# Second layer of the experts as three f32r products of split halves, with its weights split beforehand

## The reference

```python
def body(acc, ws):
    g, u, d, c = ws
    h = jax.nn.silu(x @ g.T) * (x @ u.T)
    return (acc + c[:, None] * (h @ d.T), None)
out, _ = jax.lax.scan(body, jnp.zeros_like(x), (gate_proj, up_proj, down_proj, coeff.T))
shared = jax.nn.silu(x @ shared_gate.T) * (x @ shared_up.T) @ shared_down.T
return (out + shared).reshape(B, S, Hd)
```

## Time and profile before

| | us |
|---|---|
| median of 3 runs | 1357.21 |
| lowest and highest run | 1356.95, 1358.68 |
| profiled execution | 1356.53 |
| its span | 1354.6 |
| TensorE busy in the span | 1297.6 (96%) |
| VectorE busy | 913.1 (67%) |
| ScalarE busy | 739.5 (55%) |
| GpSimd busy | 570.5 (42%) |

### The profile page before, as it was taken

How to read it: one execution, slowest core, us unless ns; L and a number is a source line. 1 busy time by engine, 2 the same in 40 slices (tenths; PEclk the granted TensorE clock), 3 DMA queues, 4 the chain that set the end, 5 groups by cost and what they waited for, 6 DMA issues and landing times.

```text
span 1354.6 us, 28636 instructions
## 1 busy us (share of the span) xinstructions
PE 1297.6 (96%) x8374; PEld 1162.2 (86%) x8374; DVE 913.1 (67%) x2131; ACT 739.5 (55%) x1688; POOL 570.5 (42%) x585
## 2 busy tenths in 40 slices
PE   7999999999999899999889999999989998989998
PEld 6898888989889797878778888988778997889996
DVE  6667666776766968687886666676767742346645
ACT  2556555565555545555546555555545654556653
POOL 5536545265330413122135546352000764656574
PEclk8999999999999899999999999999999998999999
DMA  3252645526352000000002111011157998999973
GB/s 122 87 179 85 205 142 179 178 85 205 128 182 97 28 5 28 5 28 21 13 20 67 43 62 66 27 51 54 63 188 266 393 344 302 313 383 392 390 246 113
DMA packets 128246, 195.97 MB, mean 145 GB/s; under 512 B 10400, under 2 KB 99744, under 8 KB 128160
## 3 DMA queue, kind: packets, MB, share of 16 engines
q1 hardware_dynamic: 64480, 109.77, 23.7%
q10 hardware_dynamic: 51392, 51.52, 11.2%
q0 software_dynamic: 12288, 33.57, 7.0%
HBM read 107.79 MB, written 87.03 MB: 144 GB/s over the span
## 4 chain that ended last, share of the span: by engine, by line
PE 73%; DVE 9%; issue 7%; DMA 5%; ACT 4%; SPq 1%; ACTq 0%; POOL 0%; DVEq 0%; POOLq 0%
PE ps_t L856 8%; PE ps_s L801 7%; PE ps_s L803 6%; PE ps_s L802 6%; PE ps_x L801 5%; PE ps_x L802 5%; PE ps_x L803 5%; PE ps_z L801 4%; DMA ring_down<-experts_dram 4%; PE ps_z L803 4%; PE ps_z L802 4%; PE ps_t L1021 3%; PE ps_z L1021 3%; PE ps_s L990 2%; PE ps_t L801 2%
## 5 line engine op out<-in xcount | busy, mean ns | idle before, releaser
L1133 ACT ACTIVATE prob<-prob,neg_max 128x128 f32<-128x128 f32 (+7 forms) x256 | 198.6, 776 | 243.4 <-DVE neg_max L1331 243.2
L1348 DVE TENSOR_TENSOR pT_lo<-ps_t,pT_hi 128x512 fp32r<-128x512 f32 (+2 forms) x320 | 189.5, 603 | 101.3 <-ACT pT_hi L1148 97.3
L1148 ACT ACTIVATE pT_hi<-ps_t 128x512 fp32r<-128x512 f32 (+2 forms) x320 | 161.1, 531 | 91.2 <-PE ps_t L856 91.1
L1331 DVE CUSTOM_DVE_ANT_0 prob<-ps_s,later_keys 128x128 f32<-128x128 f32 (+7 forms) x256 | 185.9, 748 | 2.4 <-PE ps_s L803 1.0
L856 PE MATMUL ps_t<-ident,prob 128*128 128x128 f32 x1152 | 172.3, 275 | 12.4 <-ACT prob L1133 5.7
L696 POOL DMA_INDIRECT xs<-xn,slots x128 | 127.7, 998 | 126.0 <-PE ps_z L1021 62.6
L856 PEld LDWEIGHTS ps_t<-ident,prob 128*128 128x128 f32 x1152 | 136.5, 141 | 39.0 <-DVE pT_lo L1348 6.7
L801 PE MATMUL ps_s<-k_hi,q_hi 128*128 128x512 f32 (+2 forms) x384 | 140.9, 367 | 1.0 <-DVE k_lo L1324 1.0
L801 PE MATMUL ps_s<-ring,a_hi 128*128 x384 | 127.0, 331 | 10.6 <-SPq L548 10.5
L1545 DVE TENSOR_TENSOR h<-sg,ps_s 128x256 f32<-128x256 f32 x112 | 47.1, 420 | 131.6 <-ACT sg L1182 131.3
L611 POOL TENSOR_TENSOR a_hi<-raw_a,zero 128x512 fp32r<-128x512 f32 x32 | 33.3, 1040 | 241.0 <-PE ps_x L803 156.0
(11 more groups left out here) (305 smaller groups left out, 3629.1 us busy)
## 6 DMA issues: line engine op xcount, KB each, us to landing
ring<-ws SPq DMA_DIRECT2D x56, 512.0 KB, 5.6
xs<-taken SPq DMA_DIRECT2D x16, 1536.0 KB, 9.7
xq<-xs ACTq DMA_DIRECT2D x48, 512.0 KB, 7.3
xs<-yq ACTq DMA_DIRECT2D x48, 512.0 KB, 7.6
ws<-split_to SPq DMA_DIRECT2D x34, 512.0 KB, 3.1
raw<-experts_dram SPq DMA_DIRECT2D x34, 256.0 KB, 3.3
raw_a<-w_a_dram SPq DMA_DIRECT2D x15, 512.0 KB, 3.7
ring_down<-experts_dram SPq DMA_DIRECT2D x56, 128.0 KB, 6.9
```

The source lines that it names most:

```text
L1133: act.activation(to, to, ACT.Exp, scale=-1.0, bias=neg_max[:, r:r + 1], accum_out=row_sum[:, c, j:j + 1]).then_inc(s_exp, 1)
L1148: act.activation(to, ps_t[m % 2][:, j * P:], ACT.Copy).then_inc(s_hi, 1)
L1331: dve.tensor_tensor_reduce(prob[r // BC][:, r % BC, 0:width(r)], ps_s[r % 2][:, first:first + width(r)], later_keys[:, S - width(r):], 1.0 ...
L1348: dve.tensor_tensor(lo, ps_t[m % 2][:, j * P:], hi.bitcast(F32), ALU.subtract).then_inc(s_bank_free, 1)
```

## The change

The second layer's weights are split together with the first layer's: `raw` takes all 768 columns of an expert, `split_to` and `ws` hold 768 high and 768 low columns, and a ring load reads high and low of both layers from `ws`, now 512 KB in rows of 2 KB and 256 KB in rows of 1 KB. `hT` becomes `hT_hi` (ScalarE's copy, in f32r) and `hT_lo` (a new subtraction on VectorE, from PSUM). TensorE's transposes of the next task, and the last second layer, wait for the low half. `down` calls `three`. To make room in SBUF the gather buffers go from 60 to 48, `coeff` shares `biased`, and two fillers go. Cut to its core:

```diff
-YQ, XQ, GATHERS = 4, 4, 60
+YQ, XQ, YG, GATHERS = 4, 4, 16, 48
...
-    ws = nc.dram_tensor("ws", [EX, P, 2 * GU], F32, kind="Internal").ap()
+    ws = nc.dram_tensor("ws", [EX, P, 2 * GU + 2 * D], F32, kind="Internal").ap()
...
-    coeff = sb("coeff", [P, NT, E])
+    coeff = biased
...
-        split_to = [sb(f"split_to{n}", [P, 2 * GU], F32R, attention) for n in range(2)]
-        raw = [sb(f"raw{n}", [P, GU], F32, attention) for n in range(2)]
-        sb("above_raw", [P, 1312], F32, attention)
+        split_to = [sb(f"split_to{n}", [P, 2 * GU + 2 * D], F32R, attention) for n in range(2)]
+        raw = [sb(f"raw{n}", [P, GU + D], F32, attention) for n in range(2)]
...
-    hT = [sb(f"hT{n}", [P, 2 * I])[:, :] for n in range(2)]
+    hT_hi, hT_lo = [[sb(f"hT_{w}{n}", [P, 2 * I], F32R)[:, :] for n in range(2)] for w in ("hi", "lo")]
...
-            sp.dma_start(ws[e], split_to[k % 2][:, 0:2 * GU].bitcast(F32)).then_inc(s_ws[k % 2], 16)
+            sp.dma_start(ws[e], split_to[k % 2][:, :].bitcast(F32)).then_inc(s_ws[k % 2], 16)
...
-                sp.dma_start(raw[k % 2][:, 0:GU], experts[e + 2][:, 0:GU]).then_inc(s_raw[k % 2], 16)
+                sp.dma_start(raw[k % 2][:, :], experts[e + 2]).then_inc(s_raw[k % 2], 16)
...
+        def by_part(t):
+
+            return t.rearrange("p (m c) -> p m c", m=2)
...
-            sp.dma_start(ring[slot].bitcast(F32), ws[which]).then_inc(s_ring[slot], 16)
-            sp.dma_start(ring_down[slot], experts[which][:, GU:]).then_inc(s_ring[slot], 16)
+            sp.dma_start(by_part(ring[slot].bitcast(F32)), by_part(ws[which])[:, :, 0:GU]).then_inc(s_ring[slot], 16)
+            sp.dma_start(by_part(ring_down[slot].bitcast(F32)), by_part(ws[which])[:, :, GU:]).then_inc(s_ring[slot], 16)
...
-            split(split_to[k % 2][:, 0:GU], split_to[k % 2][:, GU:2 * GU], raw[k % 2][:, 0:GU], count, s_pre)
+            split(split_to[k % 2][:, 0:GU + D], split_to[k % 2][:, GU + D:], raw[k % 2][:, :], count, s_pre)
...
-                pe.wait_ge(s_hT_out, g)
+                pe.wait_ge(s_hT_lo, g)
...
-                last = pe.matmul(to, hT[g % 2][:, at], downs[g][j],
-                                 start=what == "m" or j == 0, stop=what == "m" or j == 1)
+                last = three(to, hT_hi[g % 2][:, at], hT_lo[g % 2][:, at], downs[g][j][:, 0:D],
+                             downs[g][j][:, D:], what == "m" or j == 0, what == "m" or j == 1)
...
-                act.activation(hT[g % 2], ps_hT, ACT.Copy).then_inc(s_hT_out, 1)
+                act.activation(hT_hi[g % 2], ps_hT, ACT.Copy).then_inc(s_hT_out, 1)
...
+            elif kind == "B":
+                dve.wait_ge(s_hT_out, g + 1)
+                dve.tensor_tensor(hT_lo[g % 2], ps_hT, hT_hi[g % 2].bitcast(F32),
+                                  ALU.subtract).then_inc(s_hT_lo, 1)
```

More of the change, by code:

```diff
@@ L387, in build @@
     shared_gu = [sb(f"shared_gu{n}", [P, 2 * GU], F32R)[:, :] for n in range(NSH)]
-    shared_down = [sb(f"shared_down{n}", [P, D])[:, :] for n in range(NSH)]
-    down_cols = sb("ring_down", [P, RING * D])
-    ring_down = [down_cols[:, n * D:(n + 1) * D] for n in range(RING)]
+    shared_down = [sb(f"shared_down{n}", [P, 2 * D], F32R)[:, :] for n in range(NSH)]
+    down_cols = sb("ring_down", [P, RING * 2 * D], F32R)
+    ring_down = [down_cols[:, n * 2 * D:(n + 1) * 2 * D] for n in range(RING)]
     ring = [ring_cols[:, n * WC:(n + 1) * WC] for n in range(RING)]
-    later = sb("later", [P, 4 * D])
     with ExitStack() as routing:
         room_b1 = [sb(f"late_room{n}", [P, S], F32, routing) for n in range(3)]
-    yg = [sb(f"yg{n}", [P, D])[:, :] for n in range(24)]
+    yg = [sb(f"yg{n}", [P, D])[:, :] for n in range(YG)]
     yg += [t[:, d, n * D:(n + 1) * D].bitcast(F32) for t in (xT_hi, xT_lo) for d in range(ND) for n in range(S // D)]
-    yg += [t[:, n * D:(n + 1) * D] for t, count in ((later, 4), (above_ring, 4), (raw_a, 4)) for n in range(count)]
+    yg += [t[:, n * D:(n + 1) * D] for t, count in ((above_ring, 4), (raw_a, 4)) for n in range(count)]
     yg += [xn[:, t, :] for t in range(NT)]
@@ L450, in build @@
     s_gu, s_silu, s_h = sem("gu"), sem("silu"), sem("h")
-    s_hT, s_hT_out = sem("hT"), sem("hT_out")
+    s_hT, s_hT_out, s_hT_lo = sem("hT"), sem("hT_out"), sem("hT_lo")
     s_y, s_y_out, s_y_add = sem("y"), sem("y_out"), sem("y_add")
@@ L499, in _ @@
         for n in range(2):
-            sp.dma_start(raw[n][:, 0:GU], experts[n][:, 0:GU]).then_inc(s_raw[n], 16)
+            sp.dma_start(raw[n][:, :], experts[n]).then_inc(s_raw[n], 16)
             sp.sem_inc(s_ws[n], WS0)
@@ L561, in _ @@
         for n in range(NSH):
-            sp.dma_start(shared_gu[n].bitcast(F32), ws[E + n]).then_inc(s_shared, 16)
-            sp.dma_start(shared_down[n], experts[E + n][:, GU:]).then_inc(s_shared, 16)
+            sp.dma_start(by_part(shared_gu[n].bitcast(F32)), by_part(ws[E + n])[:, :, 0:GU]).then_inc(s_shared, 16)
+            sp.dma_start(by_part(shared_down[n].bitcast(F32)), by_part(ws[E + n])[:, :, GU:]).then_inc(s_shared, 16)
         sp.wait_ge(s_pv, PV0 + NP * TRS)
@@ L966, in gate_up @@
                 weights[g] = [ring_cols[:, bass.ds(a * WC, WC)] for a in at]
-                downs[g] = [down_cols[:, bass.ds(a * D, D)] for a in at]
+                downs[g] = [down_cols[:, bass.ds(a * (2 * D), 2 * D)] for a in at]
                 pe.wait_ge(s_w, second + (1 if b == 0 else 1 + E - RING))
@@ L1008, in down @@
             if g == NTASK - 1:
-                pe.wait_ge(s_hT_out, g + 1)
+                pe.wait_ge(s_hT_lo, g + 1)
             if g == 0:
```

## The result

The changed kernel takes 1375.32 us in the median (1373.63 to 1376.86, 4 runs) against 1357.36 us before: a ratio of 1.0131, 95% interval 1.0119 to 1.0143. It is 18 us slower; forecast were 1.9 us, and a range that ended at 1368. First the page of the changed kernel, its lines on the span, busy times, packets, SP's queue, and the loads of the ring (count, KB, median us from issue to landing).

What follows compares the result with a forecast made beforehand. TensorE was taken to set the pace except in early routing (VectorE) and two waits for weight loads (full DMA engines). Savings against loads and routing summed to +1.9 us: 1358.4 against 1356.53, 1359.1 as a median; range 1348 to 1368.

Steps and rivals of the forecast that it cites:

- The products: Second layer of each routed-expert task: six f32r products save 0.15 us, at most 16.8 us over 112 tasks, where TensorE leads.
- a rival: TensorE's products: weight loads set the pace, 0.38 us more per task, 42.6 us in all, 1399.8 us; chance 0.02.
- The subtraction just fits into these 0.45 us: VectorE beside routing, 1054 to 1090 us: the subtraction fits between routing step and next h; the 12.3 tasks gain nothing.
- between -1.8 and +1.8: Bounds in us on the 0 forecast for 1054 to 1090 us, 0.15 us per task either way.
- the second wait: TensorE waiting for weights, 1172.3 to 1212.8 us: 9 larger loads, 1.18 MB at 378 GB/s, +3.1 us.
- The first wait: TensorE waiting for weights, 1103.96 to 1143.5 us: 9 larger loads of 0.131 MB more at 346 GB/s, +3.4 us.
- the forecast 6.5: Larger ring loads in the two waiting stretches: 6.5 us more, as the DMA engines are full; bounds 0 and 16.0.
- Nothing that TensorE saves inside these two stretches counts: The two waiting stretches: TensorE's savings inside them bring nothing, since they end with a landing.
- The rival that the DMA engines lead there: After 1212.8 us: 14 larger loads come when wanted, +4.7 in place of 0, 1363.8 us; chance 0.14.
- The forecast's 0 for that stretch: 1212.8 to 1284 us: 0 taken between -3.6 (tasks' gain) and +4.7 (14 larger loads), as loads run ahead.
- The split and the buffers: Attention: the split's extra 7 us covered, 0. Gathers with 48 buffers: 0, at most 1.7 us.
- Queues that take turns: Ring loads: other queues keep their turns, so the waiting stretches grow by 16.0 in place of 6.5, 1368.6 us; chance 0.08.

Runs made afterwards that it cites:

- the run with routing steps behind: The changed kernel with each routing step placed behind the subtraction in VectorE's written order, not ahead of it: 1368.71 us, ratio 1.0088.
- the low half alone: The kernel before with 48 gather buffers, the subtraction and TensorE's waits for it; product still f32, loads as before, low half unused: 1364.23 us.
- the address arithmetic: The changed kernel with TensorE's addresses for gate and up worked out one step earlier, ahead of the transposes of h: 1374.32 us.
- The loads alone: The kernel before with 48 gather buffers and ring_down loaded as 256 KB instead of 128 KB, second copy unused: 1366.02 us, ratio 1.0072.
- the products alone: The changed kernel without subtraction or low-half loads, all products reading high halves; larger split and 48 gather buffers stay: 1352.09 us, ratio 0.9953.
- a third load in flight: The changed kernel with SP telling TensorE of a load two loads later, so three are in flight: 1369.50 us, ratio 1.0089.
- one transfer in fewer rows: The changed kernel with an expert's weights in one transfer of 768 KB in rows of 6 KB, 128 rows in place of 512: 1370.54 us.
- the run without the second sequence's stores: The changed kernel without the stores of the second sequence's results to HBM: 1367.17 us, ratio 1.0067.
- one run: The changed kernel with routing steps behind the subtraction, one load in rows of 6 KB and three loads in flight: 1373.46 us, ratio 1.0119.

## Why the prediction was wrong

**The products: right.** A task saves 0.15 us and takes 2.78 us where TensorE leads. With the low halves left out the products win 5.7 us. The Trainium skill (Perfetto Trace Analysis, Identifying the Most-Contended Engine) judges how much room TensorE has by the busy share of its weight loads, beside its share of peak arithmetic. As a sign of who leads the trace agrees: in the stretch of the tasks 48 to 57 they are busy for 24.88 of 25.43 us, before for 27.83 of 28.80. As a price, which the prediction made of it for a rival, it fails: six of them in place of four left a task shorter, not longer.

**The low half beside routing: wrong, and the largest error.** "The subtraction just fits into these 0.45 us" was read from one task and one gap; "between -1.8 and +1.8" bounded the lateness by what a task could win, for which there was no reason. The subtraction takes 0.416 us on the mean, as expected; but with a routing step ahead of it h, the rows' low half, the routing step and the subtraction form one chain from TensorE back to TensorE, and each second task was some 0.6 us longer. Task 13 to 32 lost 9.4 us where -1.0 was forecast. That the order was the cause is shown by the run with routing steps behind (1.2 us left there). That the full change loses 9.4 there and the low half alone 6.2 is open in part; the address arithmetic was tried and explains 0.8 us at most. Two things are on record. Without the larger loads the tasks 19 to 32 lose 4.0 us in place of 6.1; how the loads act there was not looked into. And in the tasks 13 to 19 (3.2 us lost, 2.0 with the low half alone) TensorE's clock fell, for which the forecast had no term. The rows show the changed kernel first, then the low half alone.

```profile
1039.91 0.49 PE L1004 MATMUL ps_t<-ident,h 128*128 128x128 f32 x2 [1.90 <-DVE hT_lo L1552]
1041.48 0.41 PE L803 MATMUL ps_s<-ring,a_hi 128*128 x1
1041.70 0.41 PE L804 MATMUL ps_s<-ring,a_hi 128*128 x1
...
1040.30:1043.50 3.20, 3.20 (x17) 3.20 (x17) 1.22 (x4) 0.98 (x2) 0.00 (x0) 0.50 0.94 291
...
1038.16 0.44 PE L1002 MATMUL ps_t<-ident,h 128*128 128x128 f32 x2 [1.69 <-DVE hT_lo L1550]
...
1038.00:1044.00 6.00, 5.83 (x43) 5.53 (x44) 3.85 (x11) 2.95 (x7) 0.00 (x0) 1.00 0.80 269
```

After a wait of 1.90 us for the low half the granted clock is 0.50 from 1040.30 to 1043.50 us, the lower of its two levels (1.2 GHz), and products begin 0.21 us apart in place of 0.12. For some 15 products that is 1.4 us, an estimate from these rows. In the low half alone, after a wait of 1.69 us at the same place, the clock stays at 1.00.

**The loads: right in place, too small at the second wait.** The first wait lost 3.9 for a forecast 3.4, the second 6.7 for 3.1; waits for the relay came to 22.8 where 17 were forecast. The loads alone lose 5.5 us at the two waits, near the forecast 6.5; the rest of the 10.6 goes with the other parts, as the low half alone loses 2.2 us there and the products alone 4.3. "Nothing that TensorE saves inside these two stretches counts" may be too narrow, if what is saved ahead of them is given back too; the smaller rows in that run leave this unproven. And that the 6.5 came so near is in part luck, as the loads did not only lack bandwidth, which is how the term was worked out: for the same bytes a third load in flight took back 6.6 us of the two waits, and one transfer in fewer rows 6.3.

**After 1213 us: the right resource, the wrong place.** The rival that the DMA engines lead there was to show as new waits for the relay after the second wait; there are none after 1226.7 us. That the transfers cost the time there is shown by the run without the second sequence's stores, which takes away both their bytes and their issues. The timeline at 1256.77 us shows how: through a late issue of ScalarE. That this is the whole way is not shown, as the products alone have as many late issues there and win 1.4 us. The forecast's 0 for that stretch was low by 1.3 us only, because TensorE's saving of some 3 us went there.

**The split and the buffers: right.** Attention is 0.31 us later in all; the stretch at the end, with 48 buffers, is as forecast within 0.7 us.

**Queues that take turns.** The Trainium skill (DMA: Bandwidth & Descriptors, Queues, rings and completion order) has each engine go round its queues packet by packet. No row shows the order. The changed kernel suits it: one transfer in rows of 6 KB in place of two in rows of 2 and 1 makes the waits for loads shorter (22.8 to 17.0 us) and ScalarE's issues longer (11.7 to 23.2 us) for the same bytes. The kernel before does not bear it out for the loads: rows of 5 KB left its waits at 10.5 us. The rival's 16.0 us were not reached, as the two waits lose 10.6.

In sum, the range was too narrow because each doubtful term was bounded by itself. The parts alone cost 9.4 us, inside the range (1366.8 us); together they cost 18, mostly because beside routing, where the late subtraction leads, the saving has no place (the products alone win 2.7 us there) and more is lost than by the subtraction alone.

## What to carry to other kernels

When an engine gets an instruction on which another waits, look at what stands ahead of it in the written order, not at whether its busy time has room; here moving a step by one place was worth 6.6 us. Work saved ahead of a wait that ends with a landing may be given back there (here at most 4.3 of 8.4 us), so be sure of its price only behind the last such wait. And where DMA engines are near full, look for the cost on every engine that issues transfers, not only where something waits for a load.

## What the runs showed of the hardware

An issue on ScalarE's queue, usually 0.39 us, held ScalarE for 2.43 us with the DMA engines at a share of 1.06, and in one run for 8.01 us, and the compute instructions behind it did not start until it was over (idle 1.94 and 7.47 us, put down to "issue"). The profile's list of TensorE's waits shows this as waits for VectorE's subtraction, two steps down the chain. Taking 256 KB of stores per task away made it vanish (none over 0.6 us). A full share is not enough for it: 1.05 before, with no late issue. Nor was it a collision with SP's issues: SP issued nothing from 1256.77 to 1259.20 us, and in the 8.01 us two issues of SP went by in 0.33 us each.
